# Gated feed-forward products of a two-layer transformer kernel: from two-bank pieces on VectorE to single-bank pieces of 256 columns on ScalarE and GpSimd, in other places of the program

## The reference

```python
logits = hidden @ router_w.T
top_vals, top_idx = jax.lax.top_k(logits, K)            # K = 1, N = 16 experts
...
gate_up = jnp.einsum('nth,nhf->ntf', routed_in, gate_up_proj)
gate, up = jnp.split(gate_up, 2, axis=-1)
routed_out = jnp.einsum('ntf,nfh->nth', up * jax.nn.silu(gate), down_proj)
shared = jax.nn.silu(hidden @ shared_gate_w.T) * (hidden @ shared_up_w.T) @ shared_down_w.T   # 512 wide
return (shared + expert_sum).reshape(b, s, h)
```

## Time and profile before

| what | us |
|---|---|
| median of 3 runs | 1078.5 |
| lowest, highest | 1070.91, 1096.03 |
| the profiled execution, its own time | 1067.41 |
| its span, first to last instruction | 1065.5 |

### The profile page before, as it was taken

One profiled execution on the slowest core, in us unless ns is written; L12 is line 12 of the kernel. 1 busy time (PEld: TensorE's weight loads), 2 busy tenths in 40 slices (PEclk: granted clock), 3 DMA queues, 4 the chain that ended last, 5 costly groups with the idle time before them and its releaser, 6 DMA issues.

```text
span 1065.5 us, 22648 instructions
## 1 busy us (share of the span) xinstructions
PE 922.1 (87%) x8934; PEld 339.6 (32%) x8934; DVE 887.4 (83%) x1133; ACT 819.6 (77%) x1587; POOL 185.4 (17%) x347
## 2 busy tenths in 40 slices
PE   5998888888888888888888899899988998788888
PEld 2552222222222222222232355333333453222224
DVE  7999999999999999999998688753688767797704
ACT  4139999998999998999986588574865566566786
POOL 4233300003000003000023200331032213201112
PEclk9779999999999999999999999996989999899999
DMA  3510400000000000000000451111100341100000
GB/s 108 160 52 3 134 17 16 2 2 2 1 2 2 2 2 2 2 1 2 2 2 24 133 151 53 40 46 36 37 2 4 118 126 29 41 10 1 1 11 12
DMA packets 41385, 37.03 MB, mean 35 GB/s; under 512 B 5084, under 2 KB 39452, under 8 KB 41280
## 3 DMA queue, kind: packets, MB, share of 16 engines
q1 hardware_dynamic: 39024, 30.20, 9.8%
q0 software_dynamic: 1824, 5.25, 1.7%
q10 hardware_dynamic: 432, 0.13, 0.0%
HBM read 21.92 MB, written 13.30 MB: 33 GB/s over the span
## 4 chain that ended last, share of the span: by engine, by line
PE 40%; DVE 35%; ACT 17%; issue 6%; POOL 1%; DMA 1%; another core or an unknown queue 0%; ACTq 0%; DVEq 0%; SPq 0%; POOLq 0%
DVE mx L1338 30%; ACT PT L1593 12%; PE O L1035 11%; PE T L1001 7%; PE T L1011 2%; PE S L1150 2%; PE S L966 2%; PE S L1116 2%; ACT PT L1587 1%; PE S L1106 1%; PE S L958 1%; PE T L916 1%; PE O L885 1%; PE S L971 1%; PE S L1107 1%
## 5 line engine op out<-in xcount | busy, mean ns | idle before, releaser
L1338 DVE TENSOR_REDUCE mx<-S 128x2 f32<-128x1024 f32 (+2 forms) x672 | 755.6, 1181 | 64.1 <-PE S L971 23.1
L1593 ACT ACTIVATE PT<-T 128x512 f32<-128x512 f32 (+2 forms) x1280 | 674.2, 580 | 111.0 <-PE T L1011 48.3
L1035 PE MATMUL O<-PT,Va 128*9 128x256 f32 (+1 forms) x4032 | 328.1, 390 | 5.4 <-ACT Os L1627 5.4
L1001 PE MATMUL T<-Qs,Ks 26*128 26x512 f16 x1024 | 201.5, 386 | 66.2 <-ACT PT L1593 49.8
L958 PE MATMUL S<-Ks,Qs 24*128 24x512 f16 x1024 | 201.0, 392 | 7.3 <-DVE mx L1338 3.0
L1001 PEld LDWEIGHTS T<-Qs,Ks 26*128 26x128 f16 x1024 | 55.5, 91 | 290.5 <-ACT PT L1593 191.6
L1035 PEld LDWEIGHTS O<-PT,Va 128*9 128x9 f32 x4032 | 67.6, 88 | 120.0 <-issue 109.2
L1035 PE MATMUL O<-PT,V 128*17 128x512 f32 (+3 forms) x616 | 76.2, 562 | 0.4 <-POOL PT L1772 0.3
L1011 PE MATMUL T<-Qs,K 50*128 50x512 f16 (+3 forms) x256 | 47.0, 360 | 25.3 <-ACT PT L1593 24.4
L966 PE MATMUL S<-K,Qs 48*128 48x512 f16 (+3 forms) x320 | 59.3, 363 | 7.4 <-DVE mx L1338 6.1
L1872 POOL TENSOR_SCALAR n<-nm 128x16 f16<-128x16 f32 x24 | 6.7, 280 | 309.4 <-DVE nm L1346 309.4
(11 more groups left out here) (325 smaller groups left out, 837.9 us busy)
## 6 DMA issues: line engine op xcount, KB each, us to landing
Wg<-in_L_ffn_experts SPq DMA_DIRECT2D x28, 192.0 KB, 2.5
Ks<-in_L_ffn_experts SPq DMA_DIRECT2D x20, 192.0 KB, 2.7
Vf<-sorted_x SPq DMA_DIRECT2D x12, 256.0 KB, 4.4
sorted_y<-Vf SPq DMA_DIRECT2D x12, 256.0 KB, 2.3
rows_q<-q SPq DMA_DIRECT2D x7, 256.0 KB, 2.3
sorted_x<-XP POOLq DMA_DIRECT2D x1, 1792.0 KB, 10.7
Qs<-nrow SPq DMA_DIRECT2D x96, 2.0 KB
Qs<-rows_q SPq DMA_DIRECT2D x8, 192.0 KB, 3.6
```

Source lines behind the costliest of these rows:

```text
L1001: m = e.matmul(bank, Ks[r0:r0 + 26, quad, keys], Qs[r0:r0 + 26, quad, CH * c:CH * c + CH], start=True, stop=True, tile_position=(r0, 0))
L1035: m = e.matmul(acc[32 * g:32 * g + d1, lo:hi], v, PT[(2 * j + g // 2) % 4][:, p0 + lo:p0 + hi], start=fresh, stop=True, skip_group_check=n ...
L1338: e.tensor_reduce(mx[:, u % 2, h0:h0 + 2, kb], two[:, :, 0:n], AX.X, ALU.max).then_inc(free, 1)
L1593: e.activation(PT[(2 * j + pair) % 4][:, CH * i + lo:CH * i + CH], bank[:, lo:CH], ACT.Exp).then_inc(free, 1)
```

## The change

Each gated product is now two stages, `gate` and `lift`, of 256 columns and one T bank each. ACT empties both: from the gate's bank it writes the tanh and a copy of the gate, from the lift's a copy, all to SBUF. POOL makes tanh x gate, adds gate, and multiplies with the lift. DVE has no part in it. `down` is four stages of 128 tokens with a T bank each. The three buffers are kept in two sets, so the tanh of a piece waits for POOL's result two pieces before. The planner puts a lift into the next call of `do_later` after its gate, so a gated piece takes two calls.

The places: `shared` of chunks 0 and 1 follows their own `route`, in units 5 and 6 and in units 9 and 10, one piece every 3 steps. Before, chunk 0 was done in steps 203 to 215, chunk 1 in 233 to 235 and chunk 2 in 237 to 241. Chunk 2 is now in 205 to 215. The 14 pairs of group 0, one a step before (217 to 233), now take steps 216 to 244, and the 10 of group 1, 273 to 281 before, take 273 to 287. The gathers and `setup1` hang on the last `m2`: chunk 0 of layer 1 is ready at the planner's time 255 (243 before), chunk 3 at 303 (290 before). The planner counts 344 of its own steps, 336 attention steps and 8 in which it puts out tiles alone; before it counted 336.

The diff, cut:

```diff
@@ make_plan
-        if key in ("up", "m1"):
-            P.gate[(key,) + a] = len(P.gate) + 1
+    def gated(*a):
+
+        def gate():
+            P.gate[a] = len(P.gate) + 1
+            beside("gate", *a)
+            lifts.append(a)
+        return [gate]
...
+        pieces = []
+        for p in range(n + 2):
+            if p < n:
+                pieces.append(lambda p=p: beside("m0", g, p))
+            if 0 <= p - 1 < n:
+                pieces += gated("m1", g, p - 1)
+            if 0 <= p - 2 < n:
+                pieces.append(lambda p=p: m2(p - 2))
+        pieces[-1] = lambda: (m2(n - 1), then(now[0] + 1))
+        for i, piece in enumerate(pieces):
+            at(s + i // per, piece)
 
     def shared(s, c, apart):
-        for bl in range(4):
-            at(s + apart * bl, lambda bl=bl: between("up", c, bl))
-        at(s + 4 * apart, lambda: between("down", c))
+        pieces = []
+        for half in range(2):
+            for bl in range(4):
+                pieces += gated("up", c, bl, half)
+            pieces += [lambda j=j: beside("down", c, j) for j in (2 * half, 2 * half + 1)]
+        for i, piece in enumerate(pieces):
+            at(s + int(i * apart), piece)
...
             route(t + 5, c)
+            shared(t + 10, c, 3)
...
-            shared(t + 7, 0, 3)
-            s = experts(s, 0, 1)
...
+            shared(t + 9, 2, 0.7)
...
+            experts(s, 0, 1.5, gather)
...
-            shared(t + 5, 3, 1)
...
-            s = experts(s, 1, 0.6)
...
+            shared(t + 6, 3, 0.6)
...
+            experts(s, 1, 2.3, gather)
...
         if urgent and urgent[0][0] <= now[0]:
             urgent.pop(0)[1]()
+            return
+        if lifts:
+            beside("lift", *lifts.pop())
             return
@@ pe_program
-                    e.matmul(two[:, 0, :], sgT[:, 128 * bl:128 * bl + 128], hc(c), start=True, stop=True).then_inc(gate_made, 1)
-                    e.matmul(two[:, 1, :], suT[:, 128 * bl:128 * bl + 128], hc(c), start=True, stop=True).then_inc(full, 1)
+                    bank, full = opened((name,) + tuple(a))
+                    w = sgT if name == "gate" else suT
+                    e.matmul(bank[:, 0:256], w[:, 128 * bl:128 * bl + 128], hc(c, 256 * half, 256 * half + 256), start=True, stop=True).then_inc(full, 1)
...
+                    pe.wait_ge(gated, P.gate["up", c, 3, j // 2])
...
-                    done(("m1", g, p))
+                    pe.wait_ge(gated, P.gate["m1", g, p])
@@ dv_program
-                    dv.tick(e.scalar_tensor_tensor(bt, bsg, 1.0, two[:, 0, :], ALU.add, ALU.mult))
...
-                    e.tensor_tensor(ams[bl], two[:, 1, :], bt, ALU.mult).then_inc(free, 1)
@@ ac_program
+                elif name == "gate":
+                    bank, free = filled((name,) + tuple(a))
+                    if P.gate[tuple(a)] > 2:
+                        ac.wait_ge(gated, P.gate[tuple(a)] - 2)
+                    tanh, gate, _ = gate_buffers(a)
+                    e.activation(tanh, bank[:, 0:256], ACT.Tanh, scale=0.5)
+                    e.activation(gate, bank[:, 0:256], ACT.Copy).then_inc(free, 1)
+                elif name == "lift":
+                    bank, free = filled((name,) + tuple(a))
+                    _, _, lift = gate_buffers(a)
+                    e.activation(lift, bank[:, 0:256], ACT.Copy).then_inc(free, 1)
@@ po_program
+                    po.tick(e.tensor_tensor(tanh, tanh, gate, ALU.mult))
+                    po.settle()
+                    po.tick(e.tensor_tensor(tanh, tanh, gate, ALU.add))
+                    po.settle()
+                    e.tensor_tensor(to, tanh, lift, ALU.mult).then_inc(gated, 1)
```

More of the change, by code:

```diff
@@ L350, in make_plan @@
     out = dict.fromkeys(units, 0)
-    urgent = []
+    urgent, lifts = [], []
     si = [0]
@@ L571, in make_plan @@
         J += 1
-    while later or after or light or urgent:
+    while later or after or light or urgent or lifts:
         now[0] += 1
@@ L819, in two_before, with gate_buffers @@
             return (g, p - 2) if p >= 2 else (0, GROUPS[0][3] // 2 - 2 + p) if g else None
+        def gate_buffers(a):
+            return [gates[:, P.gate[tuple(a)] % 2, i, :] for i in range(3)]
         def two_tiles(v):
@@ L1099, in pe_program @@
                     m.then_inc(full, 1)
[L1100 to L1101 removed]
+                elif name in ("gate", "lift") and a[0] == "up":
+                    _, c, bl, half = a
                     done(("turn", 1, c))
                     pe.wait_ge(ld_w1, LD_W1)
[L1104 to L1107 removed]
+                    bank, full = opened((name,) + tuple(a))
+                    w = sgT if name == "gate" else suT
+                    e.matmul(bank[:, 0:256], w[:, 128 * bl:128 * bl + 128], hc(c, 256 * half, 256 * half + 256), start=True, stop=True).then_inc(full, 1)
                 elif name == "down":
[L1109 to L1110 removed]
+                    c, j = a
+                    bank, full = opened(("down", c, j))
                     pe.wait_ge(po_scaled, SCALED["dn"])
+                    pe.wait_ge(gated, P.gate["up", c, 3, j // 2])
                     for bl in range(4):
[L1113 to L1117 removed]
+                        m = e.matmul(bank[:, 0:128], ams[bl][:, 128 * j:128 * j + 128], sdT[:, bl, :], start=bl == 0, stop=bl == 3)
                     m.then_inc(full, 1)
@@ L1139, in pe_program @@
                     m.then_inc(full, 1)
-                elif name == "m1":
-                    g, p = a
-                    _, full = opened(("m1", g, p))
-                    two = Sb[turn["m1", g, p][0]]
+                elif name in ("gate", "lift"):
+                    _, g, p = a
+                    bank, full = opened((name,) + tuple(a))
                     done(("m0", g, p))
+                    w0 = 128 * int(name == "lift")
                     for k in range(2):
@@ L1674, in ac_program @@
                     if two_before(g, p):
-                        passed(("m1",) + two_before(g, p))
+                        passed(("lift", "m1") + two_before(g, p))
                     e.activation(hS[p % 2], bank[:, 0:256], ACT.Copy).then_inc(free, 1)
-                elif name == "m1":
-                    g, p = a
-                    ac.wait_ge(gate_made, P.gate["m1", g, p])
-                    if two_before(g, p):
-                        done(("m1",) + two_before(g, p))
-                    e.activation(tS[p % 2], Sb[turn["m1", g, p][0]][:, 0, 0:256], ACT.Tanh, scale=0.5).then_inc(gate_tanh, 1)
                 elif name == "m2":
@@ L1917, in po_program @@
                     e.tensor_tensor(hv, hv, sv.unsqueeze(2).to_broadcast([128, 4, 128]), ALU.mult).then_inc(prepared, 1)
+                elif name == "lift":
+                    tanh, gate, lift = gate_buffers(a)
+                    done((name,) + tuple(a))
+                    if a[0] == "up":
+                        _, c, bl, half = a
+                        to = ams[bl][:, 256 * half:256 * half + 256]
+                        if c:
+                            passed(("down", c - 1, 2 * half + 1))
+                    else:
+                        _, g, p = a
+                        to = acS[p % 2]
+                        if two_before(g, p):
+                            passed(("m2",) + two_before(g, p))
+                    po.tick(e.tensor_tensor(tanh, tanh, gate, ALU.mult))
[3 more added lines that the diff above has]
+                    e.tensor_tensor(to, tanh, lift, ALU.mult).then_inc(gated, 1)
                 elif name == "scatter":
```

106 lines of the change are left out of this document (24 added, 82 removed).

## The result

The changed kernel takes 1156.06 us, median of 4 runs (1154.13 to 1166.95), the kernel before 1074.7 in the runs beside it (4 runs, 1063.19 to 1096.03). The ratio is 1.0824, 95% interval 1.0728 to 1.092: 8.2% slower, some 88 us, where 3.1% and 33 us were forecast. (The ratio is taken from the executions in the faster of the chip's two states alone, so it is not the quotient of the two medians, which lie 81.4 us apart.) The range (1080 to 1138) did not hold it. The profiled execution took 1166.95 us, 10.9 above its median; 9.2 of these lie ahead of step 0, which begins at 80.6 us here and at 69.8 to 71.4 in all the other profiles. They are this execution's own and no part of the change.

What follows compares the result with a forecast made beforehand. PE's queue and the banks were taken to set the pace, with DVE within 3% in the plateau. Terms 26 - 15 + 22 = +33 us on 1067.41 gave 1100.4, scaled to 1112; range 1080 to 1138.

Steps and rivals of the forecast that it cites:

- Part 1: Units 5 to 11 of layer 0: chunks 0 and 1 of the shared expert add 12.8 us each, +26 us.
- Rival A: Units 5 to 11: new pieces fall into PE's 5 us of wait per unit; +7 there, 1093 in all; chance 0.17.
- Steps 192 to 236: Late layer 0: 0 for steps 192 to 216, -18 us for 216 to 236.
- rival D: Spreading pairs does nothing; a piece costs 0.4 us wherever it is; 1108 in all; chance 0.08.
- Steps 236 to 256: End of layer 0: expert pieces, steps without tiles, setups and 16 tiles in a row make 86 us, +3.
- Steps 256 to 299: Layer 1: 0 for 256 to 280, -5 for 280 to 288, +2 us for 288 to 299 from a POOL wait.
- Steps 299 to 304: Layer 1: 41 tiles stand there instead of 13, 42 us and 1 for the chain, +28 us.
- B: Units 12 to 15 and layer 1: S banks decide, 40 turns cost 2.5 us each; -25, 1053 in all; chance 0.08.
- C: POOL becomes the queue that down, m2 and tanh wait for: ten waits of 2 us, +20 more, 1132; chance 0.12.
- The totals that were to show it: Whole kernel: DVE loses 42 us of work, ACT gains some 46, neither appearing in the forecast sum.

Runs made afterwards that it cites:

- form_only: Changed kernel with its new 256-column pieces put back at the dates of the kernel before; 1153.27 us, 1.0732 of before.
- late_ready: Kernel before, old pieces kept, with layer 1's setups 12 steps later (chunks 0 to 2) and 9 later (chunk 3); 1137.45 us, 1.0667 of before.
- on_dve: Changed kernel with the three operations of each gated piece on VectorE instead of GpSimd; 1161.89 us, 1.0887 of before.
- form_dve: New pieces at the old dates, with their three operations on VectorE instead of GpSimd; 1113.91 us in one execution, before 1066.54.
- fill_before: Kernel before with eight idle TensorE products after each step without maximum tiles in steps 236 to 303; 1065.17 us, 0.9963 of before.

## Why the prediction was wrong

**Part 1: right.** +24.5 for +26, and by its own rows: a step with a gate takes 2.81, one with a lift 2.80, against 2.22, so 0.59 and 0.58 (I took 0.6 and 0.5); one with a down 3.04, 0.82 (I took 1.0). Rival A falls. That the multiplies are hidden at three steps' distance held (no wait of PE for POOL stands in these units); they take 0.73 us, not 0.64.

**Steps 192 to 236: right**, +2.4 for 0 and -17.1 for -18. The -17.1 is no gain, though. It is work that stands later: 37 of the 56 stages of group 0 stand in these steps and 19 behind them. (66.3 less 44.6 and 1.6) over 37 is 0.54 us a piece. form_only shows that pieces of the new form are dearer when dense: a step with a pair takes 4.87, which is (4.87 - 2.23) / 4 = 0.66 a piece. So rival D, 0.4 a piece wherever it stands, is not borne out by either.

**Steps 236 to 256: the step that failed** (86 forecast, 112 measured). Three groups of its terms (some 85.5 in all) were too small, by 3.8, 9.7 and 13.1 us. First, 22 pieces at 0.25, "half hidden by PE's wait". There are 19 (56 less 37), 18 of them in steps 236 to 244, and they cost 0.6 each with the small things beside them (these steps take 31.3, eight plain ones of 2.46 are 19.7); I had 27.5 for all of it. Second, eleven steps at 2.69 plus 10 for the setups, 39.6, took 49.3 (244 to 255): I used one rate for a step without tiles, read at full clock (the plain step takes 2.46 us there and 3.75 at 1.2 GHz), and noted in the same paragraph that the clock had been 0.88 in this stretch before, as if it were a thing that goes away with the large products. It was 0.72 over the stretch. Third, the burst of 16 tiles was priced by DVE alone, 14 and 3 for the chain, and with it half a plain step, 18.3; step 255 took 31.4: DVE was busy 17.4, the chain took 4.9, and in between stand a transpose, two projections and the values of layer 1, at half clock. late_ready has the same +28.8 in these steps with the old pieces, so the new pieces are not needed for the loss: what I had priced wrongly are the late dates.

**Steps 256 to 299: failed by omission.** I put down 0 for 256 to 280, and for 288 to 299 only 2 for a wait behind the gathers. late_ready has +11.2 of the +12.3 up to 280 and +3.3 of the +7.1 without a new piece. Eight more tiles stand in 256 to 280, which I had counted and priced at nothing, and steps 256 and 257 take 5.2 and 5.1 us (2.9 and 3.5 before), with the clock still low.

**Steps 299 to 304: right in kind** (+35.4 for +28). 41 tiles took 42.7 us of DVE, and the chain 4.9 and not 1. I then took 3 us off the sum because "PE and ACT catch up a little"; nothing did.

**The rivals.** B (faster) had nothing for it; clock and S banks did decide, but against the change. C was right that POOL becomes a queue: four waits of PE, 4.6, 2.2, 4.7 and 1.0 us, in front of the downs of chunks 2 and 3, where it had ten of 2. on_dve shows that moving it gains nothing at these dates, form_dve that it costs 39 us when the pieces are dense.

**The totals that were to show it.** I had forecast 42 us less for DVE and 46 more for ACT. The 80 operations that left DVE did hold 42.3 us in the profile before. Twelve more adds come with the four-part `down`, some instructions became slower, and the sum of DVE's record durations falls by 35 us; the page shows 24 less, since it counts overlapping records once and they overlap less now (55 us against 67). For ACT the durations grow by 48 us and the page by 33.

**What the 88 us are.** By stretches: about 24 for chunks 0 and 1 in the plateau, 71 for the late dates of layer 1, 17 less in 216 to 236, and 10 or so that the old pieces at the new dates do not have, in part waits of the new ones. These shares are not prices that can be added in another order. The old form at late dates costs 71 us (late_ready), the new form at the old dates costs some 80 (form_only), and both together cost 88: spreading avoided the dense form's price and paid nearly the same for the dates. The share of the clock in the 71 is not isolated: the runs that were to do it changed the stretches as well.

No version beat the kernel before by an amount that can be told; fill_before is within 1% of it on both sides.

## What to carry to other kernels

When work is spread out, ask what waits for its last piece, not what the piece costs: here each step of delay of layer 1 cost 3 to 6 us, while pulling it forward gained nothing that could be told. A stretch that becomes thin is not cheap: its steps must be priced at the low clock as well, and both prices stand in the trace if one looks at the same instruction under either. And a rate read in a sparse place (0.25 or 0.55 us a piece) does not hold where the pieces stand close, least of all when a slow engine's queue lies between a piece and its reader.
